# Four graph layers: summing each chunk of edges into the 128 nodes from its first destination on, instead of into tiles of nodes by items

## The reference: what is computed

```
L0: Q,K,V = x W + b; score = exp(clip(sum_16(K[src] * Q[dst]) / 4, -5, 5)) for 8 heads
    h = segment_sum(score * V[src], dst) / (segment_sum(score, dst) + 1e-6)
L1: message = (x[src] + relu(edge_attr_64 W1e + b1e) W2e + b2e) / sqrt(deg[src] deg[dst]), summed over dst;
    combined = (1 + eps) x + sum, then a node MLP (W1n, W2n), + x and an RMS norm
L2: up = x W_up; message = tensor products of up[src] with the direction of edge_attr_3, weighted by an
    MLP of radial functions of edge_weight; summed over dst, / 16, times W_out
L3: a = leaky_relu(x W_src [src] + x W_dst [dst], 0.2); softmax of a over the edges of dst, per feature
    (segment max, exp, segment sum); h = segment_sum(softmax * (x W_v)[src], dst)
```

## Time and profile before

| what | value |
|---|---|
| median of 3 runs | 4919.91 us (4918.53 to 4921.03) |
| span of the profiled execution | 4919.5 us, 97134 instructions |
| PE busy | 3553.8 us, 72% |
| DVE busy | 3424.3 us, 70% |
| ACT (ScalarE) busy | 2790.1 us, 57% |
| POOL (GpSimd) busy | 3551.6 us, 72% |
| transfers | 671.22 MB, mean 136 GB/s |

### The profile page before, as it was taken

The page is one execution under the profiler, slowest core; times in us unless marked ns, Lnnn a source line. Parts: engine busy times, 40 slices in busy tenths (PEclk is TensorE's granted clock), DMA queues, the critical chain, the costliest instruction groups (busy, mean ns, idle before and its releaser), DMA issues.

```text
span 4919.5 us, 97134 instructions
## 1 busy us (share of the span) xinstructions
PE 3553.8 (72%) x21592; PEld 3017.5 (61%) x21593; DVE 3424.3 (70%) x8158; ACT 2790.1 (57%) x7271; POOL 3551.6 (72%) x3649
## 2 busy tenths in 40 slices
PE   6544444552477676767698888888888888888886
PEld 5444444442365555656576666666678888888885
DVE  5555555557554444445687777777679999999998
ACT  4777677775522222221586666666356666666665
POOL 5777777776677777777477777777557777777773
PEclk8888888886688787778889999999999999999998
DMA  7766666663433333332122222222167777777773
GB/s 216 213 210 209 208 208 211 212 213 111 116 86 80 79 81 75 86 74 59 44 58 56 57 56 56 56 57 56 42 180 215 212 211 212 212 212 212 211 212 85
DMA packets 532879, 671.22 MB, mean 136 GB/s; under 512 B 114521, under 2 KB 364991, under 8 KB 532642
## 3 DMA queue, kind: packets, MB, share of 16 engines
q0 software_dynamic: 138064, 341.31, 25.9%
q1 hardware_dynamic: 392290, 327.49, 22.4%
q10 hardware_dynamic: 2416, 1.18, 0.1%
HBM read 524.32 MB, written 85.91 MB: 124 GB/s over the span
## 4 chain that ended last, share of the span: by engine, by line
POOL 37%; issue 27%; DVE 15%; DMA 6%; PE 6%; DVEq 5%; ACT 2%; SPq 1%; POOLq 1%; ACTq 0%
POOL e_rows L972 27%; POOL acc L972 9%; DVE acc L1076 7%; DMA acc<-up_t,e_index 3%; DVEq L1081 2%; DVEq L1701 1%; PE banks L1053 1%; DVE acc L1708 1%; PE banks L525 1%; DVEq L1076 1%; PE banks L575 1%; DMA acc<-in_float_rows 1%; DMA e_rows<-kv_t,e_index 1%; PE banks L1163 1%; DVE e_top L1678 1%
## 5 line engine op out<-in xcount | busy, mean ns | idle before, releaser
L1076 DVE TENSOR_TENSOR acc<-acc,banks 128x256 f32 (+1 forms) x3520 | 1350.2, 384 | 1012.5 <-PE banks L1053 852.9
L972 POOL DMA_INDIRECT e_rows<-fsv_t,e_index x820 | 892.5, 1088 | 249.8 <-issue 214.4
L972 POOL DMA_INDIRECT e_rows<-kv_t,e_index x820 | 775.3, 946 | 249.8 <-issue 243.4
L972 POOL DMA_INDIRECT e_rows<-x_t,e_index x792 | 750.9, 948 | 256.1 <-issue 238.9
L972 POOL DMA_INDIRECT acc<-up_t,e_index x800 | 756.7, 946 | 243.8 <-issue 220.3
L1163 PE MATMUL banks<-acc,e_sel_t 128*128 x1760 | 311.9, 332 | 546.0 <-ACT e_sel_t L1149 545.7
L1313 ACT ACTIVATE e_rows<-banks,e_rows 128x128 f32<-128x128 f32 x832 | 236.3, 369 | 736.0 <-DMA e_rows<-x_t,e_index 605.4
L1163 PEld LDWEIGHTS banks<-acc,e_sel_t 128*128 128x128 f32 x1760 | 268.7, 233 | 583.5 <-issue 582.4
L1026 ACT ACTIVATE e_away<-node_iota,local 128x128 f32<-128x128 f32 x1760 | 555.1, 387 | 0.0
L1053 PE MATMUL banks<-e_rows,acc 128*128 x1760 | 516.3, 446 | 6.0 <-issue 4.2
L1304 PE MATMUL banks<-e_w,acc 65*128 65x128 f32 x1664 | 278.7, 320 | 325.9 <-DMA acc<-in_attr_rows 193.5
(11 more groups left out here) (233 smaller groups left out, 7297.7 us busy)
## 6 DMA issues: line engine op xcount, KB each, us to landing
e_near<-near_d SPq DMA_DIRECT2D x220, 258.0 KB, 4.2
sel_d<-e_sel_t SPq DMA_DIRECT2D x220, 256.0 KB
e_sel_t<-sel_d SPq DMA_DIRECT2D x220, 256.0 KB
e_far<-acc SPq DMA_DIRECT2D x880, 64.0 KB
e_resets<-reset_d SPq DMA_DIRECT2D x220, 128.0 KB
acc<-in_attr_rows SPq DMA_DIRECT2D x207, 128.0 KB
e_rows<-kv_t,e_index POOLq DMA_INDIRECT x820, 4.0
e_rows<-fsv_t,e_index POOLq DMA_INDIRECT x820
```

The source lines that it names most:

```text
L972: G.indirect_dma_start(out=self.rows[:, u, i, 0:self.width], out_offset=None, in_=self.table, in_offset=bass.IndirectOffsetOnAxis(ap=index ...
L1076: V.tensor_tensor(to, to, bank[n_bank][:, col:col + self.sums].unsqueeze(1), ALU.add).then_inc(self.s_added[i], 1)
```

## The change

It works by chunks everywhere: 208 groups in all passes, 832 chunks. A chunk's sums go to the 128 nodes from its first destination on (`base_of`, read into registers as the column in `acc`); no chunk of these edges reaches beyond 128 nodes. To be addressable at any node, `acc` is kept turned in all passes: [128 features, 2 halves, 50 x 128 nodes], and every scatter has the rows stationary and `sel` moving, two matmuls for a chunk (in e0 128 message columns and 9 others); every add covers 2 x 128 columns, in e0 too. The item tables, the slots, the late groups and e3's `head_at` go. In place of the side part there is `xt` in SBUF, and the queries of e0 and the far rows of e3 are in DRAM (`q_t`, `fdst_t`, written by `project_own` with 13 DMAs each), of which SP loads 128 rows for a chunk: new in e0 (`load_queries`), from another source in e3. The node stages read turned sums: after0 turns them back, and takes Z and deg for all nodes at once ahead of the blocks; after1 and after2 use them as they are as a matmul's stationary side. e1 has 10 slots and rounds of 10; e2 has 4 slots for messages. `near_d` is BF16 with 128 columns a chunk. Once per pass (e1, e2) the whole of `acc` is cleared, 12800 columns; before it was 6272 in e1 and 12544 in e2.

```diff
-N_GROUPS = -(-(N_CHUNKS + N_TILES - 1) // (GROUP * ROUND)) * ROUND
+N_GROUPS = -(-N_EDGES // (P * GROUP))
+N_CHUNKS = GROUP * N_GROUPS
+ROWS = (N_TILES + 1) * P
-LONG_ROUND, MSG_ROUND = 20, 16
+LONG_ROUND = 16
-    acc = sb(root, "acc", [P, N_TILES, ACC_W])
+    acc = sb(root, "acc", [P, 2, ROWS])
+    xt = sb(root, "xt", [P, N_TILES, D])
...
+            base_in = d_base.did(SP.dma_start(base_of[:, 0:USED], a["int_rows"][0:USED, 1:2].rearrange("c a -> a c")))
...
             done.append(v.did(V.tensor_tensor(xt[:, own, :], to.rearrange("p (t d) -> p t d", t=n), tiles_of(bias, n), ALU.add)))
+            wait(SP, done[-1])
+            out.did(SP.dma_start(by_tile(table)[:, own, :], xt[:, own, :]))
...
+        def sums_by_node(ctx, closing):
+            for t in range(N_TILES):
+                m = PE.transpose(turned[:, t, :], acc[0:HEADS0 + 1, 1, t * P:(t + 1) * P], ident[0:HEADS0 + 1, 0:HEADS0 + 1])
...
+                for j in range(k.size):
+                    m = PE.transpose(k.bank[0][:, j * P:(j + 1) * P], summed_tile(0, k.first + j), ident[:])
-                m = k.v.did(V.tensor_scalar(zs[:, 0, 0:k.size], acc[:, k.own, D:D + HEADS0], 1e-6, None, ALU.add))
-                mb = k.v.did(V.tensor_scalar(deg, acc[:, k.own, D + HEADS0], 1.0, None, ALU.max))
-                m = k.v.did(V.reciprocal(zs[:, 1, 0:k.size], zs[:, 0, 0:k.size]))
-                mr = k.v.did(V.reciprocal(inv, k.small[:, 3, 0:k.size]))
-                m_own = k.v.did(V.tensor_scalar(k.small[:, 2, 0:k.size], k.small[:, 3, 0:k.size], eps1[:], None, ALU.mult))
-                k.g.did(G.tensor_tensor(acc[:, k.own, 0:D], x[:, k.own, :], spread(k.small[:, 2, 0:k.size]), ALU.mult))
...
+                    PE.matmul(to, summed_tile(0, k.first + j), ident[:], start=True, stop=False)
+                    m = PE.matmul(to, summed_tile(1, k.first + j), w2e[:], start=False, stop=True)
...
-                ra = yield from k.transpose(lambda j: acc[:, k.first + j, 0:D], ht, 0)
-                rb = yield from k.transpose(lambda j: acc[:, k.first + j, D:2 * D], ht2, 1, [ra])
-                m = yield from k.project([(ht, w_out[:, 0, :]), (ht2, w_out[:, 1, :])], 0, [ra, rb])
+                    PE.matmul(to, summed_tile(0, k.first + j), w_out[:, 0, :], start=True, stop=False)
+                    m = PE.matmul(to, summed_tile(1, k.first + j), w_out[:, 1, :], start=False, stop=True)
...
-        def scatter(self, g, parts, items=range(GROUP), turned=False):
+        def scatter(self, g, parts):
+            for i in range(GROUP):
+                n_bank, col = self.place(g, i)
+                if i % 2 == 0 and g.old(2):
+                    PE.wait_ge(self.s_added[i + 1], g.upto(-2))
+                for k, rows in enumerate(parts(i)):
+                    m = PE.matmul(bank[n_bank][0:rows.shape[1], col + k * P:col + (k + 1) * P], rows,
+                                  self.place_of_sel(g)[:, i, :], start=True, stop=True)
...
-                to = acc[:, ds(self.tiles_to[i], 1), 0:self.sums]
-                V.tensor_tensor(to, to, bank[n_bank][:, col:col + self.sums].unsqueeze(1), ALU.add
+                to = acc[:, :, ds(self.bases_to[i], P)]
+                V.tensor_tensor(to, to, bank[n_bank][:, col:col + W].rearrange("p (k d) -> p k d", k=2), ALU.add
...
+            def load_queries(g):
+                bases = ps.bases(g, SP_ENGINE)
+                if not g.old(1):
+                    wait(SP, *own_made[0])
+                if g.old(QS):
+                    SP.wait_ge(s_q, g.upto(-QS))
+                for i in range(GROUP):
+                    SP.dma_start(q_rows[:, g.at(QS), i, :], q_t[ds(bases[i], P), :]).then_inc(s_q_rows[g.at(QS)], 16)
...
-                    SP.dma_start(far[:, g.r2, i, :], side(ds(tiles[i], 1)).rearrange("p a d -> p (a d)")
-                                 ).then_inc(s_far[g.r2], 16)
+                    SP.dma_start(far[:, g.r2, i, :], fdst_t[ds(bases[i], P), :]).then_inc(s_far[g.r2], 16)
...
             def scaled(g):
-                ps.tiles_to = ps.tiles(g, DVE_ENGINE)
-                _, at = nc.values_load_multi_w_load_instructions(
-                    head_at[0:1, ds(g.n, 1)], engines=(DVE_ENGINE,), min_val=0, max_val=NOWHERE,
-                    skip_runtime_bounds_check_because=CLIPPED)
+                ps.bases_to = ps.bases(g, DVE_ENGINE)
...
-                to = by_column[:, ds(at[0], 2, D)]
+                to = acc[:, :, ds(ps.bases_to[0], 1)]
                 V.tensor_scalar(to, to, shrink[:, g.r2:g.r2 + 1], None, ALU.mult).then_inc(s_scaled, 1)
```

More of the change, by code:

```diff
@@ L60 @@
 HAND_OVER = 0.15
-TO_INT = 1.5 * 2.0 ** 23
-CLIPPED = "the setup clips tiles and chunks to their tables"
-W0 = 128 + HEADS0 + 1
-W1 = 2 * D
-W2 = 256
-W3 = 256
-SIDE = 256
-ACC_W = 3 * D
-NOWHERE = (N_TILES - 1) * ACC_W + P - 1
+A_NODE = "destinations are numbers of nodes"
+W0 = D + HEADS0 + 1
+W2 = 2 * D
+W = 2 * D
 class Counter:
@@ L306, in tables @@
-        mz = v.did(V.memset(zero[:], 0.0))
-        wait(V, m, mz)
-        m = v.did(V.tensor_tensor_scan(upto[:], zero[:], count[:], 0.0, ALU.add, ALU.add))
-        wait(V, m)
-        m_upto = v.did(V.tensor_tensor(upto[:], upto[:], count[:], ALU.subtract))
-        yield PE, 0.5
-        wait(PE, m_above, m_upto)
-        PE.matmul(bank[6][:, 0:ITEM_TILES], above[:], count[:], start=True, stop=False)
-        m = pe.did(PE.matmul(bank[6][:, 0:ITEM_TILES], ones[:], upto[:], start=False, stop=True))
@@ L384, in tables @@
[L384 to L393 removed]
+        v.did(V.tensor_copy(node_iota[:], iota_i[:]))
@@ new lines, in tables @@
+        copied = []
+        for n, (lo, (of, to, end, ready)) in enumerate(itertools.product((0, GROUP), turned)):
+            hi = min(lo + GROUP, CHUNK_TILES)
+            to_bank = bank[6 + n % 2]
+            yield PE, 0.14 * (hi - lo)
+            if n == 0:
+                PE.wait_ge(made_ident, 1)
+            wait(PE, ready, *copied[n - 2:n - 1])
+            for q in range(lo, hi):
+                m = PE.transpose(to_bank[:, (q - lo) * P:(q - lo + 1) * P], of[:, q, :], ident[:])
+            m = pe.did(m)
+            end = min(end, hi * P)
+            yield V, 0.7
+            wait(V, m)
+            copied.append(v.did(V.tensor_copy(to[:, lo * P:end], to_bank[:, 0:end - lo * P])))
@@ L407, in tables @@
+        yield A, 1.0
+        wait(A, m_apart)
+        m_near = act.did(A.activation(near[:], apart[:], ACT.Copy))
         yield SP, 0.5
@@ L505, in transpose @@
             self.enter(A)
-            wait(A, m)
-            return self.act.did(A.activation(sliced(to, self), self.wide(n), ACT.Copy))
-        def turn_scaled(self, of, factors, to, n, ready):
-            yield PE, 0.25 * self.size
-            wait(PE, *ready)
-            for j in range(self.size):
-                m = PE.matmul(self.bank[n][:, j * P:(j + 1) * P], of(j), factors(j), start=True, stop=True)
-            m = self.pe.did(m)
-            yield A, 0.6
             wait(A, m)
@@ L843, in inverses @@
             wait(A, m_tiny)
-            ready = [act.did(A.activation(side(own), acc[:, own, 0:D], ACT.Ln, bias=tiny[:])) for own in blocks]
+            ready = [act.did(A.activation(xt[:, own, :], summed_tiles(0, own), ACT.Ln, bias=tiny[:])) for own in blocks]
             yield A, 0.65 * len(blocks)
@@ L945, in indices @@
                 return
-            if isinstance(g.n, int) and g.n + self.half >= self.groups:
+            if isinstance(g.n, int) and g.n + self.half >= N_GROUPS:
                 return
```

598 lines of the change are left out of this document (211 added, 387 removed).

## The result

The changed kernel takes 4659.4 us (4658.2 to 4667.2), the kernel before 4920.0: a ratio of 0.9474, with a 95% interval of 0.9462 to 0.9485. The profiled execution has a span of 4653.6 us, 265.9 less than before; the forecast was 241.7 less.

The account below looks back on a forecast made before the run. GpSimd's gather pace was taken to bound e0 and e2, and e1 apart from waits, with DVE busy for most of e3. From the profiled 4919.5 us the terms summed to -241.7, so 4678 us; range 4645 to 4745.

Parts of the forecast that it names:

- 12 groups by 5.00 us: e0's gathers: 12 groups fewer at GpSimd's pace of 5.00 us, if nothing else fills that time: -60.0 us.
- the tails: e1 and e2: 12 groups of sums after the last gather go, at 2.38 us each: -28.6 us in each pass.
- rival 2: e0 becomes bound by SP and the transfers, 5.1 to 5.55 us a group: 4700 to 4792 us; chance 15%.
- rival 3: Adds at any column cost more than 414 ns; the change is slower from 0.275 us extra per add; chance 3%.
- the gap closes, -180 x 0.20 = -36.0; bounds -45 and 0: e3's loop: without the second register load, DVE's 0.20 us gap before the scaling goes in 180 groups.
- Rival 1: e3 keeps its 5.53 us because GpSimd itself needs 5.52 us with two stretched gathers: 4714 us; chance 22%.
- three groups of adds at 0.12 us more: End of e0, after the last gather: wider adds in three groups lengthen the drain by 1.4 us.
- at most the 2.05 us that e3 takes: e0: PE's 16 matmuls per group cost at most 2.05 us, on top of 2.5 us.
- after0 gave 12.8 for 6: Stage after e0: transposes and a reciprocal added, small block operations removed: -6 us, bounds -20 and +2.
- after1 cost 5.5 for 0: Stage after e1: matmuls swapped, 13 wide DVE adds become 49 narrow ones: 0, within 6 us either way.
- after2 gave 15.4 for 9.5: Stage up to e3's first gather: 98 transposes go, -12 us; waiting for the far table in DRAM, +2.5.
- Setup was called 0: Before the first gather: item tables go, but the keys and values table is still awaited: 0, at best -5 us.

Follow-up runs that it names:

- run 7: Changed kernel with each chunk's base rounded down to a multiple of 128, so sums go to wrong nodes: 5834.5 and 5838.4 us, on slower chips.
- Run 2: Kernel before with only e3's second register load left out, scaling column 0 instead of the right one: 4855.1 us, ratio 0.9868.
- run 1: Changed kernel with e3's second register load for the scaled column put back: 4706.8 us, ratio to the kernel before 0.9564.
- run 3: Also e3_no_backward: changed kernel with e3's backward scan replaced by a product of 32 numbers: 4674.4 us.
- runs 3 and 4: The second of these: run 3's kernel with the forward scan reading logits from PSUM instead of SBUF: 5875.8 and 5880.7 us, on slower chips.
- run 5: Changed kernel with e0's second stationary part 128 columns wide instead of 9: 4655.4 us, ratio 0.9465.
- run 8: Changed kernel with e0's second part wide, acc cleared by GpSimd in after0, after1's product by ScalarE, integer table before x: 5833.4 us; repeat four_edits_b 5829.6.

## Why the prediction was right

*e0, e1's and e2's tails: right by their steps.* 12 groups by 5.00 us were 59.8, the tails 27.9 and 28.8 against 28.6. Nothing else filled e0's 5.00 us (rival 2 did not come on this chip; in the jobs on chips 8 and 1 e0's gathers took 1376 to 1392 us, bound by SP as it describes), and the add at any column is 416 ns wide, not more (rival 3; run 7).

*e3: the mechanism right, the size wrong.* The term "the gap closes, -180 x 0.20 = -36.0; bounds -45 and 0" is the one that was too small. Run 2 measures it alone as -63.6 in 200 loop groups and 20 straight ones, run 1 as +47 when put back in 180. I read the gap of 0.20 us before L1708, and did not see that L1708's own 0.32 us is 0.10 longer than in both kernels without the load (0.22). From one operation before the scaling to the one behind it the load costs 0.29 us, 0.20 of which I counted. Nor did I see that the straight code paid too. The prediction says that it has "addresses that are constants", but both loads stand in DVE's queue there as well, L1081 from 3643.12 for 0.35 us and L1701 from 3643.51 for 0.31; what it lacks are the short register operations of 0.04 and 0.06 us before them. Its bound by the two loads' distance fell short for the same reason. What is left of e3's 132 us is 68, 12 groups by 5.3 plus a drain that is 4.4 us shorter.

*Rival 1, and the rule weighed there:* the stretch was rightly laid to the scans, the conclusion "GpSimd itself needs 5.52 us" was wrong: the sum of its own times is the period in every kernel here, but the stretch in it is no constant. The argument against it, that one idle time in four is "PE banks", did not hold either: no idle time in e3 is over 0.31 us, whatever it is put down to. By run 3 a gather is held for as long as the scan that runs at its start has left, less 0.2 us; change DVE's period and other gathers meet the scans. The Trainium skill, "SBUF — State Buffer", section "SBUF: two separate sides", has a DVE operation with two SBUF inputs lock the shared ports against GpSimd until it ends; runs 3 and 4 agree in both points, the length of the hold and the two SBUF inputs. It also says that whichever starts first has the ports for its whole instruction and blocks the other. Of that half the traces show little: gathers that start up to 0.09 us after a scan are not held, and the scan is up to 0.07 us longer. A gather that starts first does not keep a scan waiting: the one at 4200.75 starts 0.13 us after a gather did, and takes 1.28 us as all others do. By these rows a gather wants the ports near its start and not for its 0.95 us.

*e0's drain:* I counted three groups of adds at 0.12 us more. There were 24 adds, six groups, after the last gather against 16 before, and that is the step that failed, at a cost of 6.8 us. The price of PE's 16 matmuls, "at most the 2.05 us that e3 takes", was wrong too: they take 2.91 us (run 5). But with that price gone the drain still has its 24 adds and 18.2 us, no less than with it within the scatter, so it is not shown to be the drain's cause. Why six groups are left where four were stays open.

*Node stages:* after0 gave 12.8 for 6, inside its bounds: DVE's busy time fell by 16.5 us, against a lead-in of 4.8 us (DVE's wait for the small transposes), so by this count nearly all of it lay on the path; no run tests that. after1 cost 5.5 for 0: its first waits show DVE held by GpSimd,

```profile
DVE after_z L637 <- POOL after_sq L625: 4.9, 2, 4.5
```

a product that I had booked as a swap without asking which engine makes it and when; run 8 won back 3.6. DVE is also busy for 77 us of the stage instead of 71, the many narrow operations, and whether the rest is that is not shown. after2 gave 15.4 for 9.5: its PE work fell by 11.8 us of the 12 forecast (69.6 to 57.8 in its window), and the 2.5 us for the far table did not show. The other 3.4 us are not explained. Setup was called 0 and cost 3.3: the load of the integer table stands behind x in SP's queue, issued from 10.8 us on, where the kernel before issued its first four integer loads from 1.0 us on; run 8 moved it ahead and won 7 to 9.

Sum of the misses: e3 -26.7, drain +6.8, after0 -6.8, after1 +5.5, after2 -5.9, setup +3.3, the rest -0.3: -24.1 us. e3 alone is more than the whole, and the others nearly cancel. That the sum of the small stages came out within 3 us is luck, since five of them missed by 3 to 7 us each.

## What to carry to other kernels

Before you read a gap, compare the next instruction's duration with its shortest in the trace: part of a wait for addresses can be booked as that duration. The distance from the start of the operation before to the start of the one behind shows the delay better than gap and excess added up, and a run without the load gives its whole price. A register load on an engine's queue is not free in a loop where this engine has no time to spare; one load that serves two uses was worth 1.3% here. When GpSimd issues indirect DMAs beside DVE scans, count on a gather held past the scan's end, and don't expect that a freer DVE makes the pass faster. Taking the scan's input from PSUM ends the hold; what it gains in time was not measured, as no run of it was made where GpSimd sets the pace.

## What the runs showed of the hardware

- An indirect gather that starts while a scan with two SBUF inputs runs takes 0.95 us plus what is left of the scan less 0.2 us, up to 1.9 us; with one input in PSUM none of 182 in each of two runs was held.
- If the gather starts within 0.09 us of the scan's start, it is the scan that gives way, by up to 0.07 us (14 times in 900 us of e3_no_backward, once in the kernel before).
- Alternating weight loads of 128 and 9 columns cost 0.06 us a matmul (16 in 2.91 us against 1.95), although the load of 9 columns alone is the shorter.
- The same program took 1.21 times as long in two jobs (5970 against 4919 us) with each compute instruction as long as ever (adds 415 and 416 ns). Single steps of SP's queue that always take 0.03 to 0.04 us in the changed kernel's e0 (the register steps between the query loads) take 0.7 us and more there in part of the cases, though a query load itself is issued in 0.33 us at the median as ever. Three lines of the chain in order of time, in four_edits_b:

```profile
307.92 0.70 issue
308.64 0.71 SPq L1026
309.35 0.73 SPq L1026
```

What slows it was not found. There the change gained less, 2.3% with the four edits.
